# A mixture-of-experts block on one core: every token through every expert, or blocks of the tokens that chose an expert

## What is computed

```
xf = h.reshape(4096, 128);  E, K, EH, SH = 8, 2, 256, 512
s = sigmoid(xf @ proj_w.T + proj_b) + expert_bias          # 8 scores per token
probs = softmax(log(clip(s)));  topk_w, topk_idx = top_k(probs, 2), weights made to sum to 1
cap = 1280                                                 # of each expert only the 1280 heaviest pairs are kept
for each expert e, each kept pair (token, weight w):
    y[token] += w * (gelu(xf[token] @ fc1_w[e].T + fc1_b[e]) @ fc2_w[e].T + fc2_b[e])
sh = gelu(xf @ sh1_w.T + sh1_b) @ sh2_w.T + sh2_b          # the shared expert, for every token
out = x + gb * (sh + y)                                    # gb: one vector of 128 per batch
```

## Time and profile before

| | us |
|---|---|
| median of three runs (lowest, highest) | 1392.53 (1389.64, 1394.34) |
| the profiled execution, its own time | 1390.22 |
| its span in the trace | 1388.5 |
| TensorE matmul busy | 1252.9 (90%) |
| VectorE busy | 1059.7 (76%) |
| ScalarE busy | 977.0 (70%) |
| GpSimd busy | 860.8 (62%) |

### The profile page before, as it was taken

The page is one execution under the profiler, slowest core; times in us unless marked ns, Lnnn a source line. Parts: engine busy times, 40 slices in busy tenths (PEclk is TensorE's granted clock), DMA queues, the critical chain, the costliest instruction groups (busy, mean ns, idle before and its releaser), DMA issues. The chain is left out here.

```text
span 1388.5 us, 31896 instructions
## 1 busy us (share of the span) xinstructions
PE 1252.9 (90%) x9674; PEld 818.7 (59%) x9674; DVE 1059.7 (76%) x1947; ACT 977.0 (70%) x2078; POOL 860.8 (62%) x1675
## 2 busy tenths in 40 slices
PE   4799999999999999999999999999995477999997
PEld 4555655656555565656565555666553355777775
DVE  3778877868777787778787777877773995788887
ACT  3677767777767776777777677777763564777776
POOL 2577667766667776677666677766746674444443
PEclk8899999999999999999999999999998798999999
DMA  5000000000000000000000000000002001434341
GB/s 133 1 2 1 2 1 2 2 4 2 1 4 2 2 1 4 2 2 2 4 2 2 4 2 2 2 2 2 1 2 77 0 0 26 122 90 101 89 94 32
DMA packets 53201, 28.60 MB, mean 21 GB/s; under 512 B 8720, under 2 KB 51224, under 8 KB 53016
## 3 DMA queue, kind: packets, MB, share of 16 engines
q1 hardware_dynamic: 51832, 25.99, 7.8%
q10 hardware_dynamic: 1184, 0.40, 0.1%
HBM read 24.16 MB, written 2.23 MB: 19 GB/s over the span
## 5 line engine op out<-in xcount | busy, mean ns | idle before, releaser
L714 ACT ACTIVATE probs<-bank,neg_max 128x512 f32<-128x512 f32 x512 | 347.2, 683 | 249.4 <-DVE neg_max L836 238.5
L836 DVE TENSOR_REDUCE neg_max<-bank 128x1 f32<-128x512 f32 x512 | 329.3, 685 | 161.0 <-PE bank L533 157.8
L573 PE MATMUL bank<-probsT,qkv 128*64 128x512 f32 x1024 | 276.2, 619 | 0.9 <-DVE oT L853 0.9
L533 PE MATMUL bank<-operands 64*128 64x512 f32 x1536 | 249.8, 430 | 1.4 <-ACT probs L714 0.9
L1003 POOL TENSOR_TENSOR inv_wide<-inv_sum,consts 128x512 f32<-128x512 f32 x64 | 66.5, 1039 | 220.9 <-DVE inv_sum L847 220.9
L549 PEld LDWEIGHTS T<-ident,probs 64*128 64x128 f32 x4096 | 170.0, 139 | 42.5 <-issue 14.7
L549 PE MATMUL T<-ident,probs 64*128 64x64 f32 x4096 | 171.1, 223 | 2.6 <-issue 1.4
L503 PEld LDWEIGHTS bank<-operands,hT_h 128*128 128x128 f32 x254 | 47.8, 188 | 209.7 <-issue 206.3
L1637 POOL TENSOR_TENSOR hid_l<-gated,hid_h 128x512 fp32r<-128x512 f32 x64 | 88.9, 1389 | 125.4 <-ACT hid_h L1554 125.4
L533 PEld LDWEIGHTS bank<-operands 64*128 64x128 f32 x1536 | 125.7, 186 | 63.3 <-issue 41.7
L842 DVE COPY probsT<-T 128x1024 f32<-128x1024 f32 x128 | 155.6, 1215 | 0.2
(11 more groups left out here) (237 smaller groups left out, 2379.2 us busy)
## 6 DMA issues: line engine op xcount, KB each, us to landing
probsT<-gate_scratch SPq DMA_DIRECT2D x64, 256.0 KB, 4.9
out<-x_all SPq DMA_DIRECT2D x8, 256.0 KB, 2.3
probsT<-in_L_ffn_fc_w SPq DMA_DIRECT2D x1, 1024.0 KB, 9.8
raw<-in_L_attn_Wq SPq DMA_DIRECT2D x1, 512.0 KB, 4.4
raw<-in_L_attn_Wk SPq DMA_DIRECT2D x1, 512.0 KB, 7.3
raw<-in_L_attn_Wv SPq DMA_DIRECT2D x1, 512.0 KB, 8.4
raw_o<-in_L_attn_Wo SPq DMA_DIRECT2D x1, 512.0 KB, 8.6
probsT<-in_L_ffn_sh_w SPq DMA_DIRECT2D x2, 256.0 KB, 2.7
```

Source lines behind the costliest of these rows:

```text
L533: last = nc.tensor.matmul(s_bank(hp, 2 * pair + head)[:], own[rows, q, toks], own[rows, k], start=((q, k) == (QH, KH)), stop=(q == QL))
L573: last = nc.tensor.matmul(O_BANK[rows, :], qkv[:, hp % 4, j, cols], probsT[:, hp % 2, head, j], start=(j == 0), stop=(j == NT - 1), skip_g ...
L714: nc.scalar.activation(probs[:, i % 4], s_bank(hp, i)[:], ACT.Exp, bias=neg_max[:, i:i + 1], accum_out=row_sum[:, hp % 2, i:i + 1]).then_i ...
L836: nc.vector.reduce_max(neg_max[:, i:i + 1], s_bank(hp, i)[:], AX.X, negate=True).then_inc(max_done, 1)
```

## The change

The third and fourth blocks become one, in which the experts see only the tokens that chose them.

In DRAM, `x_rows` has 4096 rows for each expert and 512 spare ones, each with 132 floats: a token's 128 channels, the number of the pair that it belongs to, and padding. It is filled with zeros and an impossible pair number by 13 DMAs on SP during attention. After the choices are known, VectorE computes each pair's place in its expert's region (`slots`) and GpSimd scatters the rows: 64 indirect DMAs of 128 rows. The experts' regions are cut into blocks of 512 rows; 23 blocks are always run, since no more can be needed. VectorE makes tables with the first row, the expert and the biases of each block. SP reads row and expert number of each block into registers, copies that expert's weights (4 KB per partition) within SBUF and loads the block's rows.

A block is transposed, split, sent through two hidden tiles, and transposed back, and GpSimd scatters its results to `y_rows` by pair number: 4 indirect DMAs of 128 rows, 92 in all; rows with the impossible number are dropped. At the end eight DMAs of 512 KB bring back both results of each token, and GpSimd (batches 0, 3, 6) and VectorE (the others) do `mix`: times the gates, sum of the two, times `gb`, added to the residual.

The shared expert is added to the residual on its own (`take2`, `back2`, `add_base`), its low parts move from GpSimd to VectorE, and 8 of the 15 searches run beside it. The other 7 and the gates run beside the expert blocks. The weight split stays. In the diff below, `transpose_slots` and `back` are four transposes each, `up` and `down` three matmuls each; ScalarE has `gelu` twice and a split and a `take` once for each block; `mix` is shown for VectorE and stands in the same form for GpSimd (batches 0, 3, 6). The core of the diff:

```diff
+        ROW, CHUNK, NX, NY, NW = C + 4, N, 8, 3, 4
+        CHUNKS = (EXPERTS_PER_TOKEN * T + E * (CHUNK - 1)) // CHUNK
...
+                    sp.wait_ge(s_empty, 2)
+                    for i in range(FILLS):
+                        sp.wait_ge(av_step, NT * (4 * i + 2))
+                        sp.dma_start(x_rows[5 * CHUNK * i:5 * CHUNK * (i + 1)].rearrange("(g p j) r -> p g (j r)", p=P, j=NT),
+                                     empty_rows[:].rearrange("p j r -> p (j r)").unsqueeze(1).to_broadcast([P, 5, NT * ROW])
+                                     ).then_inc(filled, 16)
...
+                    def load_weights(c, expert):
+                        after(sp, down_done, 2 * (c - NW + 1))
+                        sp.dma_start(chunk_w[:, c % NW].rearrange("p n k c -> p (n k c)").bitcast(F32),
+                                     expert_w[:, bass.ds(expert, 1)].rearrange("p o n k c -> p (o n k c)").bitcast(F32)).then_inc(w_in[c % NW], 16)
...
+                    for semaphore in first_sent:
+                        sp.wait_ge(semaphore, 16 * TT // 2)
+                    sp.wait_ge(second_sent, 16 * TT)
+                    for c in range(CHUNKS):
+                        load_weights(c, sp.value_load(weight_table[0:1, c:c + 1], min_val=0, max_val=E - 1))
+                        load_slots(c, sp.value_load(row_table[0:1, c:c + 1], min_val=0, max_val=E * T))
...
+                    for b in range(B):
+                        sp.dma_start(y_pairs[:, b].rearrange("p t k c -> p t (k c)"),
+                                     y_rows.rearrange("(b t p k) c -> b p t (k c)", b=B, t=NT, k=2)[b]).then_inc(x_in_slot[b], 16)
...
+                    def send_row(choice, t, done):
+                        nc.gpsimd.indirect_dma_start(
+                            out=x_rows, out_offset=bass.IndirectOffsetOnAxis(ap=slots[:, choice, t:t + 1], axis=0),
+                            in_=x_src[:, t], in_offset=None).then_inc(done, 16)
+
+                    def send_outputs(c):
+                        pool.wait_ge(yo_done, c + 1)
+                        for j in range(NT):
+                            nc.gpsimd.indirect_dma_start(
+                                out=y_rows,
+                                out_offset=bass.IndirectOffsetOnAxis(ap=x_slots[:, c % NX, j, C:C + 1].bitcast(U32), axis=0),
+                                in_=y_out[:, c % NY, j], in_offset=None, bounds_check=2 * T - 1,
+                                oob_is_err=False).then_inc(y_sent[c % NX], 16)
...
+                    pool.wait_ge(filled, 16 * FILLS)
+                    pool.wait_ge(slots_ready, 1)
...
+                    for half in range(2):
+                        for t in range(half * TT // 2, (half + 1) * TT // 2):
+                            send_row(0, t, first_sent[half])
+                    for half in range(2):
+                        pool.wait_ge(first_sent[half], 16 * TT // 2)
+                        number_rows(half, 1)
+                        pool.wait_ge(ids_done, 4 + half)
+                        for t in range(half * TT // 2, (half + 1) * TT // 2):
+                            send_row(1, t, second_sent)
+                    for c in range(CHUNKS):
+                        send_outputs(c)
...
+                    for s in range(CHUNKS + 3):
+                        if s < CHUNKS:
+                            transpose_slots(s)
+                        if 0 <= s - 1 < CHUNKS:
+                            up(s - 1, 0)
+                            up(s - 1, 1)
+                        if s in SEARCH_STEPS:
+                            count(SEARCH_STEPS[s])
...
+                        if 0 <= s - 2 < CHUNKS:
+                            down(s - 2, 0)
+                            down(s - 2, 1)
+                        if 0 <= s - 3 < CHUNKS:
+                            back(s - 3)
...
+                    def gelu(c, k):
+                        n = 2 * c + k
+                        act.wait_ge(up_ready, n + 1)
+                        after(act, hl_done, n - 3)
+                        nc.scalar.activation(act_out[:, n % 4], H_BANK[k][:], ACT.Gelu,
+                                             bias=bias_of[:, c, k:k + 1]).then_inc(gelu_done, 1)
+                        act.wait_ge(gelu_done, n + 1)
+                        after(act, down_done, n - 3)
+                        nc.scalar.activation(hid_h[:, n % 4], act_out[:, n % 4], ACT.Copy).then_inc(hh_done, 1)
...
+                    for c in range(B):
+                        for k in range(SHT):
+                            n = SHT * c + k
+                            if k == 0:
+                                search_first(c)
+                            dve.wait_ge(hi2_done, n + 1)
+                            nc.vector.tensor_tensor(hid_l[:, k], act_out[:, k], hid_h[:, k].bitcast(F32),
+                                                    ALU.subtract).then_inc(lo2_done, 1)
+                            if k == 1 and c > 1:
+                                add_base(c - 2)
+                            if k == 2:
+                                search_last(c)
...
+                    def take_rows(c):
+                        dve.wait_ge(yt_ready, c + 1)
+                        if c >= NY:
+                            semaphore, value = sent(c - NY)
+                            dve.wait_ge(semaphore, value)
+                        nc.vector.tensor_copy(y_out[:, c % NY], BACK_BANK[:].rearrange("p (j c) -> p j c", j=NT)).then_inc(yo_done, 1)
...
+                    def mix(b, n):
+                        dve.wait_ge(*pairs_there(b))
+                        rows = y_pairs[:, b]
+                        by = gate2[:, b * NT:(b + 1) * NT].unsqueeze(3).to_broadcast([P, NT, 2, C])
+                        nc.vector.tensor_tensor(rows, rows, by, ALU.mult).then_inc(mix_step, 1)
+                        dve.wait_ge(mix_step, 3 * n + 1)
+                        nc.vector.tensor_tensor(rows[:, :, 0], rows[:, :, 0], rows[:, :, 1], ALU.add).then_inc(mix_step, 1)
...
```

More of the change, by code:

```diff
@@ L167, in adaln_attention_moe @@
             s_const = sem("s_const")
+            s_empty = sem("s_empty")
             x0_in = sem("x0_in")
@@ new lines, in adaln_attention_moe @@
+            rt = sem("rt")
+            consts = sem("consts")
+            xsrc_ready = sem("xsrc_ready")
+            xsrc_done = sem("xsrc_done")
+            ids_done = sem("ids_done")
+            diag_done = sem("diag_done")
+            gb_ready = sem("gb_ready")
+            gb_copied = sem("gb_copied")
+            sel_ready = sem("sel_ready")
+            pos_out = sem("pos_out")
+            slots_ready = sem("slots_ready")
+            first_sent = [sem(f"first_sent{i}") for i in range(2)]
@@ new lines, in adaln_attention_moe @@
+            y2_taken = sem("y2_taken")
+            z2_ready = sem("z2_ready")
+            base_done = sem("base_done")
+            x_in_slot = [sem(f"x_in_slot{i}") for i in range(NX)]
+            w_in = [sem(f"w_in{i}") for i in range(NW)]
+            y_sent = [sem(f"y_sent{i}") for i in range(NX)]
+            xt_ready = sem("xt_ready")
+            xh_done = sem("xh_done")
+            xl_done = sem("xl_done")
+            up_ready = sem("up_ready")
+            gelu_done = sem("gelu_done")
@@ new lines, in weight_bank @@
+            def weight_bank(j):
+                whole = bank[j % 4][:]
+                return whole.unsqueeze(1) if j < 2 else whole.rearrange("p (e n) -> p e n", e=2)
+            GROUPS = 2 * TILES // 4
+            LAG2 = 2
+            H_BANK, Y_BANK, BACK_BANK, XT_BANKS = bank[0:2], bank[2], bank[3], bank[4:6]
+            COUNT_BANK, FIN_BANK = bank[6], bank[7]
+            SHARED_SEARCHES = B
+            SEARCH_STEPS = {2 * i + 1: SHARED_SEARCHES + i for i in range(SEARCHES - SHARED_SEARCHES)}
@@ new lines, in adaln_attention_moe, with pairs_there, mixed @@
+            FINAL_STEP = 2 * (SEARCHES - SHARED_SEARCHES) + 1
+            POOL_BATCHES = (0, 3, 6)
+            assert FINAL_STEP < CHUNKS
+            assert NX == B
+            DVE_BATCHES = tuple(b for b in range(B) if b not in POOL_BATCHES)
+            def pairs_there(b):
+                return x_in_slot[b], 16 * (len(range(b, CHUNKS, NX)) + 1)
+            def mixed(b):
+                return (out_pool, POOL_BATCHES.index(b) + 1) if b in POOL_BATCHES else (out_dve, DVE_BATCHES.index(b) + 1)
@@ new lines, in gates @@
+                        link(nc.vector.tensor_tensor(above[:], above[:], by_expert(prob), ALU.mult))
+                        for k, choice in enumerate((top1, top2)):
+                            link(nc.vector.tensor_tensor(t1[:], choice[:], above[:].rearrange("p e t -> p t e"), ALU.mult))
+                            last = nc.vector.reduce_sum(gate2[:, :, k], t1[:], AX.X)
+                            if k == 0:
+                                link(last)
+                        last.then_inc(gates_done, 1)
@@ new lines, in _ @@
+                    for s in range(CHUNKS + 3):
```

(19 more changed lines are left out.)

1022 lines of the change are left out of this document (523 added, 499 removed).

## The result

On the chip of the first measurement the changed kernel took 1434.2 us, median of 4 (1433.0 to 1445.9), against 1393.0 for the kernel before: ratio 1.032, interval 1.026 to 1.038. This is 64 us above the forecast of 1370, inside the range of 1318 to 1450, and slower where faster was the likelier.

| chip | changed kernel, us | range | ratio to before | kernel before, us |
|---|---|---|---|---|
| first measurement | 1434.2 | 1433.0-1445.9 | 1.032 [1.026, 1.038] | 1393.0 |
| 8 | 1379.3 | 1378.0-1380.9 | 0.992 [0.991, 0.994] | 1389.7 |
| 5 | 1439.1 | 1433.9-1443.6 | 1.035 [1.031, 1.038] | 1390.5 |
| 0 | 1380.7 | 1378.1-1383.3 | 0.993 [0.990, 0.995] | 1391.1 |
| 2 | 1454.0 | 1440.2-1455.7 | 1.042 [1.036, 1.048] | 1392.6 |

A forecast was written before the change was run, and what follows sets the result against it. The old expert stage was bound by its 768 matmuls, becoming 276; GpSimd's sends then pace. Scatter landed 1189, first send 1205, blocks 129 us to 1334, span 1366, plus 1.7 and 2.3: 1370 us, range 1318 to 1450.

The forecast's parts named there:

- Ahead of the shared expert: Before the shared expert: weight groups end at 1090.4, `slots` ready at about 1097.5, first low part at 1108, 9 us lost.
- The disputed term, X: GpSimd's time per indirect send of 128 rows, taken as 1.4 us; all sends cost it 156 X.
- The shared expert beside the scatter: Shared expert ends at 1171; the scatter beside it ends at 1187 and lands at 1189, with 18 us exposed.
- a sign of being wrong: The forecast called itself wrong if, among other signs, the shared expert ended after the scatter.
- a doubt for VectorE's interfaces: GpSimd shares SBUF interfaces with VectorE; whether a send suffers no row shows; it would lie on the dear side.
- The dear rival: In the sends: each holds GpSimd 2.0 us, making it the bound for good; 1464 us; chance 0.28.
- From the first load to the first send of results: First block: loads 4.4 us, then one pass through all engines, about 10 us; first send at 1189 + 16 = 1205.
- The blocks: Expert blocks: GpSimd paces at 5.6 us per block, 23 x 5.6 = 129 us, to 1334.
- The rival of the low clock: Expert blocks: TensorE at low clock paces at 7.0 us a block, 32 more, 1402 us; chance 0.06, shared with other paces.
- The tail: After the last send: landed 1336, first results back 1340, GpSimd's and VectorE's mixes end near 1363, span 1366.

The follow-up runs named there:

- f3: The changed kernel, but GpSimd waits for each row send to land before it issues the next; 1460.5 us.

## Why the prediction was right or wrong

The chips without stalls show how good the sum was; on chip 8 the span is 1377.7 against 1366 forecast. The chip of the first measurement shows the term that the sum lacked.

- *Ahead of the shared expert*: in the first measurement the weight groups ended at 1092.2 (1090.4 forecast) and `slots` was ready at 1099.7 (1097.5), on chip 8 each 1.3 us later; the first send began at 1100.7 and 1102.0. Late by 2 to 4.5 us.
- *The disputed term, X*: right in kind and high by 0.1. First measurement, the sends (line, busy us, mean ns, idle before by cause):

```profile
L1317 POOL DMA_INDIRECT x_rows<-x_src,slots x64 | 64.1, 1002 | 25.7 <-issue 25.7
L1324 POOL DMA_INDIRECT y_rows<-x_src,probsT x92 | 93.5, 1016 | 117.0 <-DVE x_src L1776 88.8 <-issue 28.2
```

  1.00 us and 0.30 of issue make 1.3 us against 1.4. That is the same with stalls and without, and the scatter (1100.7 to 1184.3; 1102.0 to 1186.2 on chip 8; 1187 forecast) was never late. The Trainium skill's 2.0 us for a DMA from GpSimd ("DMA: Bandwidth & Descriptors", Anatomy of one DMA — SWDGE (gpsimd) path) did not hold the engine, as its sentence on the receipt suggests; f3, which waits for each landing, has one send per 2.6 us (167 us for 64).
- *The shared expert beside the scatter*: on chip 8 the first load of a block starts at 1188.6, forecast 1189, with the last down product's end at 1173.2 against 1171. In the first measurement this product is at 1224.5, 40 us behind the end of the scatter, which the prediction had named as a sign of being wrong. **This is the step that failed**: the prediction let the sends run "beside the shared expert" and charged them only to GpSimd's own time, with a doubt for VectorE's interfaces. It put what they cost TensorE's hand-over at nothing, without a reason. Measured, TensorE's increments come up to 26 us late while the sends run, and with it the first load stands 37 us later and the blocks take 18 us more. No term, and no rival, held that sends could go with late increments of an engine that doesn't take part in them. The dear rival had the sign (1464) for another reason, a longer X, which the sends' rows refute; that 1434 lies inside the stated range is luck, for the range's upper part stood for that X.
- *From the first load to the first send of results*: 24.8 us where 16 was taken. The loads took 4.2 us, as forecast; the pass took 20.6 instead of some 11.6. Two things that the prediction left out are in chip 8's rows:

```profile
1192.81 1.08 PE L1466 MATMUL T<-ident,probsT 128*128 128x128 f32 x4 [18.12 <-DMA probsT<-x_rows]
...
1203.16 0.63 PE L1475 MATMUL bank<-operands 128*128 128x512 f32 x1
...
1211.23 0.60 PE L1492 MATMUL T<-ident,y_cols 128*128 128x128 f32 x4
```

  TensorE had been idle and works at the low clock until 1204.4, 15 matmuls at 0.43 us instead of 0.23, some 3 us. And the first block isn't alone: in TensorE's fixed order the transposes of the next three blocks, the up products of two, two counts and the down products of one stand ahead of `back` of block 0. Its `take` ended at 1206.4, and `back` began at 1211.2, 4.8 us later.
- *The blocks*: 125.8 us against 129, GpSimd without idle time in most of them, as forecast; 143.9 in the first measurement. The rival of the low clock didn't come about: on chip 8 the granted clock is 0.91 to 1.00 in each 20 us from 1210 to 1310.
- *The tail*: 38.5 us from the last send, 32 forecast. The mixes were priced by rows of 512 columns on other operands. On chip 8, VectorE's product of 1024 columns and sum of 512 beside GpSimd's mixes and after them:

```profile
1352.59 2.91 DVE L1819 TENSOR_TENSOR probsT<-probsT,gate 128x1024 f32<-128x1024 f32 x1
...
1355.54 1.63 DVE L1821 TENSOR_TENSOR probsT<-probsT 128x512 f32<-128x512 f32 x1
...
1368.28 1.21 DVE L1819 TENSOR_TENSOR probsT<-probsT,gate 128x1024 f32<-128x1024 f32 x1
1369.52 0.69 DVE L1821 TENSOR_TENSOR probsT<-probsT 128x512 f32<-128x512 f32 x1
```

  2.4 times slower with GpSimd beside it, where 1.4 times was taken: 7.8 us for a batch instead of 4.9. (The Trainium skill's "GPSIMD Engine Reference", Specifications, names contention where a VectorE instruction has two SBUF inputs, as these have; the trace agrees.) GpSimd's three batches took 7.7 us each. VectorE alone would need 8 x 3.3 = 26.4 us for all eight against the 30.3 that both took (1344.7 to 1375.0); that is an estimate, and it wasn't tried.

Sum for chip 8: -0.4 at the first load, +8.8 for the first pass, -3.2 for the blocks, +6.5 for the tail, 11.7 us of span; the median is 1.6 us above the span instead of 4.0, hence 1379.3 where 1370 stood. Terms too small by 15.3 us and too large by 3.6 went into it, so the 9 us flatter it a little. Where there are stalls, 37 and 18 us come on top.

**Shown**: the two times belong to the chip or its state at the time, not to single executions. All five traces with the long time have late increments of TensorE, in the shared expert and in the blocks, and none of the ten others with indirect sends has one; so both the 37 and the 18 us go with them. On one chip that has them, direct sends by GpSimd for 34 us brought none, and indirect ones did. A bounds check changes nothing.

**Open**: what distinguishes the chips; what holds TensorE's increments back and what lets them go. One rival no run has touched: the traces with late increments are also those that lack most landing increments, and every execution on record has its span and clock from the recorder beside its time. So the recording itself may have a part in the stalls, and whether the program has them when nothing is recorded is not known.

## What to carry to other kernels

Work of GpSimd that seems free beside TensorE isn't proven free by its own length: look, in the profile of the changed kernel, at how long after its matmul the consumer starts. When a pipeline is filled by a fixed instruction order, price the first result with all that stands ahead of it in that order, at the clock of an engine that comes from idle. And before a cause is sought in a program, run it again unchanged beside the first experiments: here eleven runs told little about the stalls, because the changed kernel hadn't stood beside them on their chips.

## What the hardware showed that was not expected

- With indirect sends running, TensorE's increments came up to 26 us late on the chip of the first measurement, 45 on chip 2, and late ones stood on chips 5 and 13 too; none on chips 1, 7, 3, 8 and 0. Those of ScalarE and VectorE were never over 0.02 us late. The kernel before takes 1389.7 to 1393.0 us on all of them.
- GpSimd's drain at the end of the block lasts 9.24 us in the changed kernel, whose list holds 64 and 92 indirect sends, and 1.57 us in the kernel before, which has none; what makes it long no run isolates.
- An indirect send of 128 rows of 512 or 528 bytes holds GpSimd 0.96 to 1.02 us plus 0.27 to 0.30 of issue; a direct one of 128 rows of 528 bytes 0.53 to 0.55 us.
- GpSimd's mixes slow VectorE's float32 sums of two operands from 0.69 to 1.63 us.
